# Three edits to a post-norm transformer layer: half order in the first projection slab, attention writes by quarters, smaller loads

## The chip, the cores and the metric

One Trainium2 chip, all 8 cores. The metric is the time of the slowest core in microseconds (us). Each core works on its own data: one of 4 sequences, and half of its query rows. No data passes between cores.

## What is computed

The reference, cut to its core (4 sequences of 4096 rows, width 4096, 32 heads of 128, 8 KV heads, 8 LoRA adapters of rank 16):

```python
q = (x @ Wq + bq); k = (x @ Wk + bk); v = (x @ Wv + bv)      # k, v repeated 4 times over heads
scores = einsum('bhqd,bhkd->bhqk', q, k) / sqrt(128) + causal_mask
attn   = einsum('bhqk,bhkd->bhqd', softmax(scores), v)
x = layernorm(x + attn @ Wo + bo)
h = einsum('bsd,nrd->nbsr', x, lora_A)
x = layernorm(x + x @ W.T + bias + einsum('nbsr,nor->bso', h, lora_B * coef))
```

## The kernel before

The kernel is raw code without a scheduler: each operation is written down once for its engine with the operations that it depends on, and each engine runs its operations in the order in which they were written. That holds for DMA issues too. An engine (SP, ACT or GpSimd, which the profile calls POOL) that issues a DMA first waits in its own queue for what the DMA depends on, and all that is queued behind it waits as well. A phase (`ir.phase`) begins on every engine only when the last operation of each engine and of each DMA channel of the phases before has finished. PE is TensorE, DVE is VectorE.

*Projection stage* (`gen_gemm`, L246 to L341). It is run for K and V over two groups of 2048 rows of x, and then once for Q over the core's 2048 query rows. A group of x (`x_bf`, 128 x 32 x 2048 in bf16) is loaded by GpSimd's queue in two halves of 1024 rows, 16 loads each (L259). The loads of a half wait for the last matmul that read the same half of the group before (`pe_last_half`, L255), and at most four are in flight. Weights come in slabs of four chunks (512 columns) into one buffer `w_bf`, in 8 loads (L284), queued behind the x loads of the group. K and V have four slabs, Q has eight. Odd groups run the slabs in reverse order, so that the first slab of the second K/V group is the last of the first and isn't loaded again. PE's work on a slab is a list of pairs (chunk, half), L294 to L298. Each pair is a pass over 32 row chunks of the contraction, with 2 matmuls of 128x512 for each, 64 in all. In most slabs the two halves follow each other within a chunk. In the last slab of a group all chunks of half 0 come first, so that the loads of the next group's half 0 can start.

*Attention stage* (L350 to L534). Four q blocks `qt` of 512 rows, for each of them 32 heads, for each head `NK = 8 * (qt + 1)` key chunks `kc`. A step is one score matmul (L466), the exponential on ACT (L471), for the last 8 chunks a mask multiply on DVE (L478), and, three steps late (`LAG = 3`), the matmuls with V (L452) and for the denominator (L455). A head's last three V matmuls therefore stand among the first three score matmuls of the next head. Two tails of each head run in the next one: after its third step the denominator is copied (L493) and inverted, and in the fifth step a matmul spreads it over the partitions (L506), ACT copies it (L510) and DVE multiplies it in (L514), into `aslab[:, h * 512:(h + 1) * 512]`.

SP's queue issues for this stage: the q load of each head (L433, two buffers, so that the load of head h + 2 waits for the last score matmul of head h), in q block 0 the K load of each of the 8 KV groups (L375, 1 MB), and the V chunks. These are loaded by a transposing DMA, one for each KV group and key chunk (L382), when they are first needed: 8 for each KV group in every q block, at the group's first head (0, 4, 8, ...). A transpose of one KV group waits for the transpose before it in that group (`vt_prev`). After a q block's last tail SP issues one write of all of `aslab` (4 MB) to `a_dram` (L528), then the mask (L414) and the q load of the next block. DVE's multiply into `aslab` waits for the last such write.

*Output stage* (L536 to L885), for two groups `tg` of 1024 query rows. `attnT` (8 MB) is loaded back in four loads of 2 MB (L664), and the first matmul (L680) waits for all four. The projection with Wo follows (L692), with residual, row sums and sums of squares, and a write of the sum to `r1_dram`. The first normalisation loads row blocks of 128 rows (2 MB, L740, two buffers), normalises them (L744) and transposes them on PE (L752). The LoRA and feed-forward matmuls (L771, L817, L824) follow, with a write to `r2_dram`. The second normalisation loads each row block in two halves of 1 MB from ACT's queue (L864), normalises each half (L873) and writes it to `y` (L879). Both belong to ACT's queue, so the loads of the next row block are issued only after both writes of this one, which wait for both multiplies.

Of the kernel before, what the change touches and what calls it, by code (L numbers as in the profile page):

```python
# [11 lines left out]
ALU = mybir.AluOpType  # L12
# [99 lines left out]
def build_program(cfg):  # L112
    T, D, H, KVH = cfg["T"], cfg["D"], cfg["H"], cfg["KVH"]
# [41 lines left out]
    ir = IR()  # L155
# [90 lines left out]
    def gen_gemm(src, gcount, gt, nsub, chunks, oc_base, same_layout=False):  # L246
# [5 lines left out]
        for gi in range(gcount):  # L252
# [21 lines left out]
            for slab in slabs:  # L274
# [16 lines left out]
                        for d in dset:  # L291
                            wc_ops[d] = ld
                new_lastuse = {}
                is_last_slab = (slab is slabs[-1])  # L294
                if is_last_slab:
                    pairs = [(ci, half) for half in range(halves) for ci in range(len(slab))]
                else:
                    pairs = [(ci, half) for ci in range(len(slab)) for half in range(halves)]  # L298
# [106 lines left out]
    rtmm_last = {}  # L405
    av_par = {}
    tail_prev = [None]
    slab_wr = [None]
    mask_last = [None]
    b_attn_done = None  # L410

    for qt in range(NQT):
# [17 lines left out]
        for h in range(H):  # L430
# [57 lines left out]
            def make_tails(h=h, hp=hp, stopv=stopv):  # L488
                carry = {}

                def tail1():
                    stopDen = stopv[1]
                    dc = ir.op("dve", lambda e, hp=hp: e.tensor_copy(  # L493
                        out=den_sb[hp][:], in_=ps_den[hp][:]), deps=[stopDen, lnlast.get(0)])
                    dclast[0] = dc
                    ln1 = ir.op("act", lambda e, hp=hp: e.activation(
                        out=rec_sb[hp][:], in_=den_sb[hp][:], func=AF.Ln), deps=[dc, rtmm_last.get(0)])
                    dr = ir.op("act", lambda e, hp=hp: e.activation(
                        out=rec_sb[hp][:], in_=rec_sb[hp][:], func=AF.Exp, scale=-1.0),
                        deps=[ln1])  # L500
                    lnlast[0] = dr
                    carry["dr"] = dr

                def tail2():
                    stopAV = stopv[0]
                    rt = pe_op(lambda e, hp=hp: e.matmul(  # L506
                        ps_rt[hp][:], orf_sb[:], rec_sb[hp][:], start=True, stop=True),
                        [carry["dr"], d_orf, rt_evac.get(0)])
                    rtmm_last[0] = rt
                    re = ir.op("act", lambda e, hp=hp: e.activation(  # L510
                        out=rt_sb[hp][:], in_=ps_rt[hp][:], func=AF.Identity),
                        deps=[rt, at_evac.get(0)])
                    rt_evac[0] = re
                    ae = ir.op("dve", lambda e, h=h, hp=hp: e.tensor_tensor(  # L514
                        out=aslab[:, h * 512:(h + 1) * 512], in0=ps_av[hp][:],
                        in1=rt_sb[hp][:], op=ALU.mult), deps=[stopAV, re, slab_wr[0]])
                    av_par[hp] = ae
                    at_evac[0] = ae
                return tail1, tail2
            t1, t2 = make_tails()  # L520
            tails.append([LAG, t1])
# [3 lines left out]
        for tset in tails:  # L525
            tset[1]()
        tails.clear()
        sw = ir.op("sp", lambda e, qt=qt: e.dma_start(  # L528
            out=a_dram[qt], in_=aslab[:]),
            deps=[av_par.get(0), av_par.get(1)], dma=True, chan="sw")  # L530
        slab_wr[0] = sw
        b_attn_done = sw
    freeall(psg)
    freeall(gb)  # L534

# [117 lines left out]
    for tg in range(NTG):  # L653
# [3 lines left out]
        for i in range(TSG):  # L657
            t, g = ps(f"psc{tg}_{i}", [128, 512]); pscg.append(g); psc.append(t)
        atld = []
        W2 = H * 512 // 2  # L660
        for qh in range(TG // 512):
            qt = tg * (TG // 512) + qh
            for hv in range(2):
                atld.append(ir.op("sp", lambda e, qt=qt, qh=qh, hv=hv: e.dma_start(  # L664
                    out=attnT[:, qh * H * 512 + hv * W2:qh * H * 512 + (hv + 1) * W2],
                    in_=a_dram[qt, :, hv * W2:(hv + 1) * W2]),
                    deps=[slab_wr[0], last_ffn_mm[0]],
                    dma=True, chan=f"atld{len(atld)}"))

        for oc in range(NOC):  # L670
# [66 lines left out]
        for ts in range(TSG):  # L737
            slot = ts % 2
            rows = tg * TG + ts * 128
            ld = ir.op("sp", lambda e, rows=rows, slot=slot: e.dma_start(  # L740
                out=rowbuf[slot][:], in_=r1_dram[rows:rows + 128, :]),
                deps=r1_done + rowbuf_user.get(slot, []), dma=True, chan=f"row{slot}")
            fin = ln1_fin
            xb = ir.op("dve", lambda e, ts=ts, slot=slot: e.tensor_scalar(  # L744
                out=x1row[:], in0=rowbuf[slot][:], scalar1=stat_rstd[:, ts:ts + 1],
                scalar2=stat_mb[:, ts:ts + 1], op0=ALU.mult, op1=ALU.add),
                deps=fin + [ld, x1row_waw[0]])
            rowbuf_user[slot] = [xb]
            lasttr = None
            for Dc in range(DC):  # L750
                i2 = ts * DC + Dc
                tr = pe_op(lambda e, Dc=Dc, i2=i2: e.transpose(  # L752
                    tp2[i2 % 2][:], x1row[:, Dc * 128:(Dc + 1) * 128], id_sb[:]),
                    [xb, d_id, x1f_ev.get(i2 - 2)])
                evv = ir.op("dve", lambda e, Dc=Dc, ts=ts, i2=i2: e.tensor_copy(
                    out=x1f[:, Dc * TG + ts * 128:Dc * TG + (ts + 1) * 128], in_=tp2[i2 % 2][:]),
                    deps=[tr])
                x1f_ev[i2] = evv
                lasttr = tr
            x1row_waw[0] = lasttr  # L760
# [98 lines left out]
        for ts in range(TSG):  # L859
            slot = ts % 2  # L860
            rows = tg * TG + ts * 128
            lds = []
            for hv in range(2):
                lds.append(ir.op("act", lambda e, rows=rows, slot=slot, hv=hv: e.dma_start(  # L864
                    out=rowbuf[slot][:, hv * D2:(hv + 1) * D2],
                    in_=r2_dram[rows:rows + 128, hv * D2:(hv + 1) * D2]),
                    deps=r2_done + [c2_xc_last[0]] + rowbuf_user.get(slot, []),
                    dma=True, chan=f"row{slot}" if hv == 0 else f"row{slot}b"))
            fin = ln2_fin
            oa2 = []  # L870
            for hv in range(2):
                osl = (ts * 2 + hv) % 3
                oa = ir.op("dve", lambda e, ts=ts, slot=slot, hv=hv, osl=osl: e.tensor_scalar(  # L873
                    out=outst[osl][:], in0=rowbuf[slot][:, hv * D2:(hv + 1) * D2],
                    scalar1=stat_rstd[:, ts:ts + 1],
                    scalar2=stat_mb[:, ts:ts + 1], op0=ALU.mult, op1=ALU.add),
                    deps=fin + [lds[hv]] + (outlast.get(osl) or []))
                oa2.append(oa)
                ow = ir.op("act", lambda e, rows=rows, hv=hv, osl=osl: e.dma_start(  # L879
                    out=y[rows:rows + 128, hv * D2:(hv + 1) * D2],  # L880
                    in_=outst[osl][:]),
                    deps=[oa], dma=True, chan=f"out{osl}")
                outlast[osl] = [ow]
                out_wr.append(ow)
# [65 lines left out]
```

How the kernel before makes its waits and increments, by code:

```python
                    def body(e, ids=ids):  # L95
                        waited = {}
                        for i in ids:
                            o = self.ops[i]
                            for d in o["deps"]:
                                p = self.ops[d]
                                if waited.get(p["sem"].num, -1) < p["val"]:
                                    e.wait_ge(p["sem"], p["val"])
                                    waited[p["sem"].num] = p["val"]
                            if o["fn"] is not None:
                                inst = o["fn"](e)
                                if o["sig"] or o["dma"]:
                                    inst.then_inc(o["sem"], 16 if o["dma"] else 1)
```

## Time and profile before

| | us |
|---|---|
| timed runs of before | 7345.82 and 7667.84, median 7506.83 |
| profiled execution | 7378.19 |
| its span, slowest core (core 3) | 7376.6 |
| spans of the other cores | 7326.0 to 7367.9 |
| PE busy in the span | 6164.9 (84%) |
| ACT, DVE, POOL busy | 2021.9, 915.7, 355.6 |

All shown rows are of core 3. The span runs from the first to the last instruction. The projection stage ends at about 2198, the q blocks begin at about 2199, 2545, 3010 and 3679, and attention ends at about 4570; the output stage of the first row group runs to about 6057.

### The profile page before, as it was taken

Reading aid. Unit: us, or ns where it says so; the run is one execution under the profiler, and the core shown is the slowest. Engines: PE = TensorE matmul, PEld = TensorE weight load, DVE = VectorE, ACT = ScalarE, POOL = GpSimd, SP = SyncE. Lnnn points to the kernel's source line nnn. Section 1 sums busy time; section 2 is a strip of 40 time slices with the busy share of each in tenths; the row PEclk is TensorE's granted clock in tenths of the full one; section 3 lists DMA queues with packets and bytes.
Section 4 is the critical chain, followed back from the end, with each engine's and each line's share of the span. In section 5 each row is a group of like instructions: output and inputs, shape, how many; then the busy total and the mean of one; then the engine's idle time right before and its main releaser. Section 6 shows DMA issues by size and latency. Waiting matters only on the chain.

```text
span 7376.6 us, 76089 instructions; the slowest of 8 cores (7326.0 to 7376.6 us)
## 1 busy us (share of the span) xinstructions
PE 6164.9 (84%) x25344; PEld 2271.1 (31%) x25344; DVE 915.7 (12%) x2390; ACT 2021.9 (27%) x3873; POOL 355.6 (5%) x480
## 2 busy tenths in 40 slices
PE   2988995999988899899999997789598849868883
PEld 0433442444432122222222221333243313323331
DVE  0000000000002222111111110111411111132111
ACT  0000000000014467677667775000011100001110
POOL 1001001000000000000000000000000000000000
PEclk9998997999996699999999998899699969978996
DMA  8246337323221100100000002666356696654667
GB/s 117 40 63 106 62 54 111 58 45 59 44 49 44 58 15 16 35 10 11 25 16 9 8 7 69 139 113 126 123 110 128 129 273 109 128 150 88 127 127 214
DMA packets 421434, 593.31 MB, mean 80 GB/s; under 512 B 75299, under 2 KB 316996, under 8 KB 408132
## 3 DMA queue, kind: packets, MB, share of 16 engines
q0 software_dynamic: 224704, 247.51, 24.7%
q10 hardware_dynamic: 101376, 201.37, 8.2%
q1 hardware_dynamic: 94980, 139.57, 5.7%
q8 instruction: 219, 3.59, 0.2%
q14 instruction: 155, 1.27, 0.1%
HBM read 676.42 MB, written 150.99 MB: 112 GB/s over the span
## 4 chain that ended last, share of the span: by engine, by line
PE 70%; DMA 20%; DVE 5%; issue 4%; SPq 0%; DVEq 0%; ACT 0%; ACTq 0%; POOL 0%; POOLq 0%
PE pa L309 18%; PE psd L817 12%; PE psd L692 10%; PE ps_den L455 9%; PE ps_s L466 9%; PE ps_av L452 7%; DMA w_bf<-wq 3%; DMA rowbuf<-r_scr 3%; DMA x_bf<-xt_kv 3%; DMA v_sb<-v_scr 2%; PE ps_rt L506 2%; DMA w_bf<-wk 2%; DMA w_bf<-wo 2%; DMA x_bf<-xt_q 1%; DMA w_bf<-wv 1%
## 5 line engine op out<-in xcount | busy, mean ns | idle before, releaser
L309 PE MATMUL pa<-x_bf,w_bf 128*128 128x512 bf16 x8192 | 1832.3, 386 | 361.6 <-DMA w_bf<-wk 167.1
L471 ACT ACTIVATE pt_sb<-ps_s 128x512 bf16<-128x512 f32 (+3 forms) x2560 | 1337.8, 531 | 615.8 <-PE ps_s L466 601.4
L309 PEld LDWEIGHTS pa<-x_bf,w_bf 128*128 128x128 bf16 x8192 | 804.4, 99 | 1389.0 <-issue 468.1
L452 PE MATMUL ps_av<-pt_sb,v_sb 128*128 128x512 bf16 (+3 forms) x2560 | 929.0, 363 | 109.2 <-DVE den_sb L493 85.7
L466 PE MATMUL ps_s<-q_sb,k_sb 128*128 128x512 bf16 (+3 forms) x2560 | 950.5, 372 | 62.9 <-DMA q_sb<-q_scr 48.9
L692 PE MATMUL psd<-w_bf,attnT 128*128 128x512 bf16 x4096 | 936.0, 392 | 46.7 <-DMA w_bf<-wo 46.4
L817 PE MATMUL psd<-w_bf,x1f 128*128 128x512 bf16 x4096 | 919.0, 388 | 4.9 <-DMA w_bf<-wff 4.8
L455 PE MATMUL ps_den<-pt_sb,ocol_sb 128*1 128x512 bf16 (+3 forms) x2560 | 912.5, 356 | 0.0
L478 DVE TENSOR_TENSOR pt_sb<-pt_sb,mask_sb 128x128 bf16<-128x128 bf16 x1024 | 230.1, 225 | 3619.9 <-ACT pt_sb L471 3614.6
L692 PEld LDWEIGHTS psd<-w_bf,attnT 128*128 128x128 bf16 x4096 | 408.0, 100 | 574.7 <-issue 129.0
L817 PEld LDWEIGHTS psd<-w_bf,x1f 128*128 128x128 bf16 x4096 | 405.8, 100 | 517.7 <-issue 59.5
L455 PEld LDWEIGHTS ps_den<-pt_sb,ocol_sb 128*1 128x1 bf16 x2560 | 202.5, 79 | 954.3 <-issue 951.6
L466 PEld LDWEIGHTS ps_s<-q_sb,k_sb 128*128 128x128 bf16 x2560 | 246.0, 96 | 674.6 <-issue 631.9
L714 ACT ACTIVATE scr_bf<-rst 128x512 bf16<-128x512 f32 x128 | 80.8, 631 | 1059.6 <-DVE rst L703 1052.0
L321 ACT ACTIVATE estage<-pa,bq_sb 128x512 bf16<-128x512 f32 x128 | 88.1, 688 | 966.4 <-PE pa L309 933.9
L844 ACT ACTIVATE scr_bf<-rst 128x512 bf16<-128x512 f32 x128 | 80.8, 631 | 901.7 <-DVE rst L833 897.3
L452 PEld LDWEIGHTS ps_av<-pt_sb,v_sb 128*128 128x128 bf16 x2560 | 254.6, 99 | 153.3 <-issue 152.2
L680 PE MATMUL psd<-bo_bc,orb_sb 1*128 1x512 bf16 x128 | 63.3, 517 | 234.1 <-DVE rst L703 130.3
L752 PE MATMUL tp<-id_sb,x1row 128*128 128x128 bf16 x512 | 106.7, 265 | 170.4 <-DVE x1row L744 89.6
L833 DVE TENSOR_TENSOR rst<-psd,xres 128x512 f32<-128x512 f32 x128 | 87.3, 682 | 964.3 <-PE psd L824 964.3
L703 DVE TENSOR_TENSOR rst<-psd,xres 128x512 f32<-128x512 f32 x128 | 87.3, 682 | 943.3 <-PE psd L692 935.3
L321 ACT ACTIVATE estage<-pa,bv_sb 128x512 bf16<-128x512 f32 x64 | 44.1, 689 | 470.6 <-PE pa L309 453.7
(62 smaller groups left out, 1758.5 us busy)
## 6 DMA issues: line engine op xcount, KB each, us to landing
w_bf<-wo POOLq DMA_DIRECT2D x128, 512.0 KB, 6.1
r_scr<-rst ACTq DMA_DIRECT2D x256, 256.0 KB, 7.2
w_bf<-wff POOLq DMA_DIRECT2D x128, 512.0 KB, 5.7
x_bf<-xt_kv POOLq DMA_DIRECT2D x64, 512.0 KB, 12.4
w_bf<-wq POOLq DMA_DIRECT2D x64, 512.0 KB, 7.7
xres<-x_q ACTq DMA_DIRECT2D x128, 256.0 KB, 6.4
rowbuf<-r_scr SPq DMA_DIRECT2D x16, 2048.0 KB, 8.5
xres<-r_scr SPq DMA_DIRECT2D x128, 256.0 KB, 7.9
```

Of the source, the lines that this page charges most:

```text
L309: mm = pe_op(lambda e, bank=bank, Dc=Dc, ci=ci, half=half, sub=sub, gt=gt, gth=gth: e.matmul(pa[bank][:], w_bf[:, Dc * 512 + ci * 128:Dc * ...
L321: act = ir.op("act", lambda e, bank=bank, slot=slot, bias_sb=bias_sb, bias_i=bias_i: e.activation(out=estage[slot][:], in_=pa[bank][:], fu ...
L452: av = pe_op(lambda e, kc=kc, kv=kv, par=par, hp=hp, NK=NK, s=s: e.matmul(ps_av[hp][:, s:512], v_sb[:, kc * DKV + kv * 128:kc * DKV + (kv ...
L455: dn = pe_op(lambda e, kc=kc, par=par, hp=hp, NK=NK, s=s: e.matmul(ps_den[hp][:, s:512], ocol_sb[:], pt_sb[par][:, s:512], start=(kc == 0) ...
L466: mm = pe_op(lambda e, kc=kc, kv=kv, par=par, hp=hp, s=s: e.matmul(ps_s[par][:, s:512], k_sb[:, kv * T + kc * 128:kv * T + (kc + 1) * 128] ...
L471: ex = ir.op("act", lambda e, par=par, s=s: e.activation(out=pt_sb[par][:, s:512], in_=ps_s[par][:, s:512], func=AF.Exp, scale=ISQ), deps= ...
L478: cur = ir.op("dve", lambda e, par=par, c=c, s=s: e.tensor_tensor(out=pt_sb[par][:, s:s + 128], in0=pt_sb[par][:, s:s + 128], in1=mask_sb[ ...
L506: rt = pe_op(lambda e, hp=hp: e.matmul(ps_rt[hp][:], orf_sb[:], rec_sb[hp][:], start=True, stop=True), [carry["dr"], d_orf, rt_evac.get(0)])
L692: mm = pe_op(lambda e, f=f, fi=fi, ts=ts, wi=wi, acol=acol: e.matmul(psc[ts][:], attnT[:, acol:acol + 128], w_bf2[wi % 2][:, fi * 512:(fi ...
L703: ev = ir.op("dve", lambda e, ts=ts, slot=slot: e.tensor_tensor(out=rst[slot][:], in0=psc[ts][:], in1=xres[slot][:], op=ALU.add), deps=[st ...
L752: tr = pe_op(lambda e, Dc=Dc, i2=i2: e.transpose(tp2[i2 % 2][:], x1row[:, Dc * 128:(Dc + 1) * 128], id_sb[:]), [xb, d_id, x1f_ev.get(i2 - 2)])
L817: mm = pe_op(lambda e, f=f, fi=fi, ts=ts, wi=wi: e.matmul(psc[ts][:], x1f[:, f * TG + ts * 128:f * TG + (ts + 1) * 128], w_bf2[wi % 2][:, ...
```

## The change

First, the first slab of a K/V group after the first, and of the Q group, is ordered like the last slab: all chunks of half 0, then all of half 1. Second, `aslab` is written in four quarters (8 heads, 1 MB each, each with its own channel). A quarter's write is issued by SP in the tail of its last head (7, 15, 23, 31), and the multiply waits only for the write of its own quarter. Third, three loads are cut: `attnT` into eight pieces instead of four, the row block of the first normalisation into two instead of one, and that of the second into four instead of two.

```diff
-                is_last_slab = (slab is slabs[-1])
-                if is_last_slab:
+                is_first_after = (slab is slabs[0]) and (gi > 0 or same_layout)
+                if (slab is slabs[-1]) or is_first_after:
                     pairs = [(ci, half) for half in range(halves) for ci in range(len(slab))]
                 else:
                     pairs = [(ci, half) for ci in range(len(slab)) for half in range(halves)]
...
-    slab_wr = [None]
+    swq = {}
+    slab_wr_q = {}
+    QD = max(H // 4, 1)
...
-                def tail2():
+                def tail2(qt=qt):
...
+                    qd = h // QD
                     ae = ir.op("dve", lambda e, h=h, hp=hp: e.tensor_tensor(
                         out=aslab[:, h * 512:(h + 1) * 512], in0=ps_av[hp][:],
-                        in1=rt_sb[hp][:], op=ALU.mult), deps=[stopAV, re, slab_wr[0]])
+                        in1=rt_sb[hp][:], op=ALU.mult), deps=[stopAV, re, swq.get(qd)])
                     av_par[hp] = ae
                     at_evac[0] = ae
+                    if h % QD == QD - 1:
+                        w = ir.op("sp", lambda e, qt=qt, qd=qd: e.dma_start(
+                            out=a_dram[qt, :, qd * QD * 512:(qd + 1) * QD * 512],
+                            in_=aslab[:, qd * QD * 512:(qd + 1) * QD * 512]),
+                            deps=[ae, swq.get(qd)], dma=True, chan=f"sw{qd}")
+                        swq[qd] = w
+                        slab_wr_q.setdefault(qt, []).append(w)
...
-        sw = ir.op("sp", lambda e, qt=qt: e.dma_start(
-            out=a_dram[qt], in_=aslab[:]),
-            deps=[av_par.get(0), av_par.get(1)], dma=True, chan="sw")
-        slab_wr[0] = sw
-        b_attn_done = sw
+        b_attn_done = slab_wr_q[qt][-1]
...
-        W2 = H * 512 // 2
+        W2 = H * 512 // 4
...
-            for hv in range(2):
+            for hv in range(4):
                 atld.append(ir.op("sp", lambda e, qt=qt, qh=qh, hv=hv: e.dma_start(
...
-                    deps=[slab_wr[0], last_ffn_mm[0]],
+                    deps=slab_wr_q[qt] + [last_ffn_mm[0]],
...
-            ld = ir.op("sp", lambda e, rows=rows, slot=slot: e.dma_start(
-                out=rowbuf[slot][:], in_=r1_dram[rows:rows + 128, :]),
-                deps=r1_done + rowbuf_user.get(slot, []), dma=True, chan=f"row{slot}")
+            lds = []
+            for hv in range(2):
+                D2 = D // 2
+                lds.append(ir.op("sp", lambda e, rows=rows, slot=slot, hv=hv, D2=D2: e.dma_start(
+                    out=rowbuf[slot][:, hv * D2:(hv + 1) * D2],
+                    in_=r1_dram[rows:rows + 128, hv * D2:(hv + 1) * D2]),
+                    deps=r1_done + rowbuf_user.get(slot, []), dma=True,
+                    chan=f"row{slot}" if hv == 0 else f"row{slot}b"))
...
-                deps=fin + [ld, x1row_waw[0]])
+                deps=fin + lds + [x1row_waw[0]])
...
-            for hv in range(2):
-                lds.append(ir.op("act", lambda e, rows=rows, slot=slot, hv=hv: e.dma_start(
-                    out=rowbuf[slot][:, hv * D2:(hv + 1) * D2],
-                    in_=r2_dram[rows:rows + 128, hv * D2:(hv + 1) * D2]),
+            D4 = D // 4
+            for qv in range(4):
+                sub = "bcd"[qv - 1] if qv else ""
+                lds.append(ir.op("act", lambda e, rows=rows, slot=slot, qv=qv: e.dma_start(
+                    out=rowbuf[slot][:, qv * D4:(qv + 1) * D4],
+                    in_=r2_dram[rows:rows + 128, qv * D4:(qv + 1) * D4]),
                     deps=r2_done + [c2_xc_last[0]] + rowbuf_user.get(slot, []),
-                    dma=True, chan=f"row{slot}" if hv == 0 else f"row{slot}b"))
+                    dma=True, chan=f"row{slot}{sub}"))
...
-                    deps=fin + [lds[hv]] + (outlast.get(osl) or []))
+                    deps=fin + lds[2 * hv:2 * hv + 2] + (outlast.get(osl) or []))
```

The second edit moves instructions in SP's queue. The piece below is of q block 0, from the K load of heads 8 to 11 on. Before:

```order
L375 DMA k_sb<-k_scr 128x4096
L382 DMA_TRANSPOSE v_sb<-v_scr 128x128 x5
L433 DMA q_sb<-q_scr 128x512
L382 DMA_TRANSPOSE v_sb<-v_scr 128x128 x3
L433 DMA q_sb<-q_scr 128x512 x3
L375 DMA k_sb<-k_scr 128x4096
```

And with the change, where the line numbers are two higher and L523 is the new write:

```order
L375 DMA k_sb<-k_scr 128x4096
L382 DMA_TRANSPOSE v_sb<-v_scr 128x128 x2
L523 DMA a_scr<-aslab 128x4096
L382 DMA_TRANSPOSE v_sb<-v_scr 128x128 x3
L435 DMA q_sb<-q_scr 128x512
L382 DMA_TRANSPOSE v_sb<-v_scr 128x128 x3
L435 DMA q_sb<-q_scr 128x512 x3
```

The write of heads 0 to 7 stands between the second and the third of the eight V transposes of the KV group that begins with head 8. The q load behind the next three transposes is that of head 9.

In q block 1, from the transposes of heads 4 to 7 to those of heads 8 to 11, SP's queue before:

```order
L382 DMA_TRANSPOSE v_sb<-v_scr 128x128 x5
L433 DMA q_sb<-q_scr 128x512
L382 DMA_TRANSPOSE v_sb<-v_scr 128x128 x3
L433 DMA q_sb<-q_scr 128x512 x3
L382 DMA_TRANSPOSE v_sb<-v_scr 128x128 x5
L433 DMA q_sb<-q_scr 128x512
```

And with the change:

```order
L382 DMA_TRANSPOSE v_sb<-v_scr 128x128 x5
L435 DMA q_sb<-q_scr 128x512
L382 DMA_TRANSPOSE v_sb<-v_scr 128x128 x3
L435 DMA q_sb<-q_scr 128x512 x3
L523 DMA a_scr<-aslab 128x4096
L382 DMA_TRANSPOSE v_sb<-v_scr 128x128 x5
L435 DMA q_sb<-q_scr 128x512
L382 DMA_TRANSPOSE v_sb<-v_scr 128x128 x3
```

Here the write stands ahead of all eight transposes, because only key chunks 8 to 15 are new in this block. The last of the three q loads ahead of it is that of head 8, and the same holds at heads 16 and 24, and in q blocks 2 and 3. At the end of a q block the order is as before, with a quarter of `aslab` in place of the whole.

## Rows read from the trace of the kernel before

**Rows 1.** The page's first line, and its waits of one group of matmuls (part 5).

```profile
span 7376.6 us, 76089 instructions; the slowest of 8 cores (7326.0 to 7376.6 us)
...
L466 PE MATMUL ps_s<-q_sb,k_sb 128*128 128x512 bf16 (+3 forms) x2560 | 950.5, 372 | 62.9 <-DMA q_sb<-q_scr 48.9
```

**Rows 2.** Timeline from 587 us (start, us, engine, line, op; idle before and its releaser).

```profile
587.46 0.69 ACT L321 ACTIVATE estage<-pa,bv_sb 128x512 bf16<-128x512 f32 x1 [11.87 <-PE pa L309]
...
601.27 0.69 ACT L321 ACTIVATE estage<-pa,bv_sb 128x512 bf16<-128x512 f32 x1 [11.87 <-PE pa L309]
...
629.63 0.71 POOL L259 DMA_DIRECT2D x_bf<-xt_kv  x1 [6.26 <-PE pa L309]
...
643.95 1.02 PE L309 MATMUL pa<-x_bf,w_bf 128*128 128x512 bf16 x4 [0.25 <-DMA x_bf<-xt_kv]
...
690.83 89.07 PE L309 MATMUL pa<-x_bf,w_bf 128*128 128x512 bf16 x404 [0.60 <-DMA x_bf<-xt_kv]
```

**Rows 3.** Timeline of SP's queue, q block 0, transposes of heads 8 and 16.

```profile
2281.83 14.98 SPq L382 DMA_TRANSPOSE v_sb<-v_scr  x5
...
2298.03 5.63 SPq L382 DMA_TRANSPOSE v_sb<-v_scr  x3
...
2364.65 12.76 SPq L382 DMA_TRANSPOSE v_sb<-v_scr  x5
```

**Rows 4.** Timeline of DVE and PE in the same stretch.

```profile
2300.17 0.69 DVE L514 TENSOR_TENSOR aslab<-ps_av,rt_sb 128x512 bf16<-128x512 f32 x1 [1.44 <-ACT rt_sb L510]
...
2304.94 0.26 PE L452 MATMUL ps_av<-pt_sb,v_sb 128*128 128x128 bf16 x1 [0.50 <-DMA v_sb<-v_scr]
```

**Rows 5.** Timeline of SP's queue, q blocks 1, 2 and 3 (first and last of a head).

```profile
2662.43 10.14 SPq L382 DMA_TRANSPOSE v_sb<-v_scr  x5
2675.43 0.32 SPq L433 DMA_DIRECT2D q_sb<-q_scr  x1
...
2690.69 27.14 SPq L433 DMA_DIRECT2D q_sb<-q_scr  x3
...
3184.47 0.33 SPq L433 DMA_DIRECT2D q_sb<-q_scr  x1
...
3204.64 40.65 SPq L433 DMA_DIRECT2D q_sb<-q_scr  x3
...
3908.09 0.33 SPq L433 DMA_DIRECT2D q_sb<-q_scr  x1
...
3935.01 55.66 SPq L433 DMA_DIRECT2D q_sb<-q_scr  x3
```

**Rows 6.** Timeline of DVE, the normalising multiply of heads 7 in q blocks 1 and 2.

```profile
2682.22 0.69 DVE L514 TENSOR_TENSOR aslab<-ps_av,rt_sb 128x512 bf16<-128x512 f32 x1 [3.73 <-ACT rt_sb L510]
...
3190.68 0.69 DVE L514 TENSOR_TENSOR aslab<-ps_av,rt_sb 128x512 bf16<-128x512 f32 x1 [3.52 <-ACT rt_sb L510]
```

**Rows 7.** Timeline around the end of q block 0.

```profile
2546.30 8.24 SPq L433 DMA_DIRECT2D q_sb<-q_scr  x1
...
2559.27 1.86 PE L466 MATMUL ps_s<-q_sb,k_sb 128*128 128x512 bf16 x4 [15.44 <-DMA q_sb<-q_scr]
```

**Rows 8.** A window after that end: stretch, us, busy by engine, PEclk, DMA share, GB/s.

```profile
2559.00:2565.00 6.00, 5.73 (x13) 1.10 (x14) 0.00 (x0) 3.26 (x6) 0.00 (x0) 0.51 0.05 11
```

**Rows 9.** DMA issues (part 6): line, count, KB each, median us to landing.

```profile
rowbuf<-r_scr SPq DMA_DIRECT2D x16, 2048.0 KB, 8.5
...
k_sb<-k_scr SPq DMA_DIRECT2D x8, 1024.0 KB, 5.9
```

**Rows 10.** Chain that ended last, end of the attention stage: start, us, what.

```profile
4569.86 12.58 DMA a_scr<-aslab
```

**Rows 11.** Timeline of the last normalising stage, first row blocks.

```profile
7262.22 0.81 ACTq L864 DMA_DIRECT2D rowbuf<-r_scr  x2
7268.83 1.35 DVE L873 TENSOR_SCALAR outst<-rowbuf,stat_rstd,stat_mb 128x2048 f32<-128x2048 f32 x1 [7.17 <-DMA rowbuf<-r_scr]
...
7271.99 1.35 DVE L873 TENSOR_SCALAR outst<-rowbuf,stat_rstd,stat_mb 128x2048 f32<-128x2048 f32 x1 [1.81 <-DMA rowbuf<-r_scr]
```


## The prediction

> **What bounds the kernel now.** I read the page first, then the waits, the chain that ended last, and the timeline at each place where the chain leaves TensorE (PE). PE is the bound nearly everywhere in a span of 7376.6 us [rows 1]. A change that leaves every matmul in place can win only where PE stands still, and lose only where it makes PE stand still. The reader is to see four such places. (a) In the projection stage PE waits for the second half of the next x: it begins that half's first matmuls at 643.95 and meets the last load at 690.83 [rows 2]. (b) At each of the three changes of q block PE waits for the first q. One of the three waits is 15.44 us [rows 7], and together they make nearly all of the 48.9 that this group waits for q [rows 1]. (c) The attention stage ends with one write of 4 MB, 12.58 us on the chain [rows 10]. (d) Both normalising stages at the end of a token group run at the pace of loads and stores [rows 11].
>
> The fifth place is one where PE does not wait today. SP's queue carries the q loads, the K loads, the transposed V loads and the attention writes in one line. In a group of four heads it runs a head ahead: in q block 1 the five transposes of head 8 start at 2662.43, while the head's own scores begin only about 2675.4 [rows 5].
>
> **The change part by part.** All is summed on the profiled execution's 7378.19 us (span 7376.6), which lies between the two timed runs, 7345.82 and 7667.84, whose median is 7506.83.
>
> *First slab by halves.* One pass (a chunk of one half, 64 matmuls) takes 601.27 - 587.46 = 13.81 us [rows 2]. Before, PE starts the half-1 pass at 643.95 and needs until 690.83 + 1.7 = 692.5, the last load's four matmuls included. With the change three more half-0 passes come first, 643.9 to 685.3, and the half-1 pass then runs to 699.1. The last load's matmuls are due at the end of that pass, at 698.2, 7 us after it has landed. The stall 692.5 - 643.95 - 13.8 = 34.7 us is gone; nothing is late next. The same order at the start of the Q projection gives nothing. There the weight loads stand behind all 32 x loads in GpSimd's queue, so no pass can start before both halves of x are loaded or on their way. I take 35 us, bounds 30 to 35.
>
> *Writes by quarters, at the ends of q blocks.* The first q of the next block no longer queues behind 4 MB but behind 1 MB, plus the mask. 4 MB take 12.58 us [rows 10], 1 MB takes 5.9 us as the K loads show [rows 9]: 6.7 us less. By the slope alone (12.58 / 4 = 3.1 us a MB) it would be 9.4. Three changes of block at 7 us give 21 (bounds 15 to 29), and the end of the stage gives 6.7 (5 to 9.4).
>
> *Writes by quarters, inside a q block.* The writes after heads 7, 15 and 23 of every block now stand in SP's line behind a wait for the multiply of that head (L514), which comes in the fifth step of heads 8, 16 and 24. Each of these heads is the first of a new KV group, so behind the waiting write stand the group's V transposes, six of eight in q block 0 and all eight in the others, and between them the q load of the next head. A transpose waits for the one before, five in 10.14 us, 2.05 each [rows 5]. Behind a 1 MB K load in the same queue five took 14.98 and 12.76 [rows 3], so 1 MB ahead costs 2.6 to 4.8 us. I take 3.7 for the write.
>
> - q block 0: L514 ends at 2300.86 [rows 4]; write issued by 2301.3; three transposes 3 x 2.05 + 3.7, to 2311.1. From the end of the fifth transpose (2281.83 + 14.98) to the end of the last three (2298.03 + 5.63) are 6.85 us [rows 3], so 2318.0. PE took the last V at 2304.94, 1.3 after its issue ended [rows 4]; now it is 2319.3. Stall 14.3 us.
> - q block 1: L514 ends at 2682.91 [rows 6]; transposes from 2683.3; 10.14 + 3.7, q load 0.4, three more 5.7, landing 1.3: 2704.5. The head's scores ended at 2690.69 [rows 5] and the last V is due three steps later, at 2693.2 (a step is (3935.01 - 3908.09) / 32 = 0.84 us). Stall 11.3.
> - q block 2: L514 ends at 3191.37, 6.9 after the head's start at 3184.47 [rows 5, 6]; the same 21.2 us from 3191.8 give 3213.0. Due at 3204.64 + 2.5 = 3207.1. Stall 5.9.
> - q block 3: the same offset gives 3908.09 + 7.3 + 21.2 = 3936.6, due at 3937.5. No stall, 0.9 us of cover.
>
> Three each: 3 x 31.5 = 94.5 us. While PE is paced by the transposes it is mostly idle, and after an idle stretch its clock is low: in the 6 us after the wait at 2559.27 the granted clock is 0.51 of full, 1.2 GHz [rows 7, 8], 6 x 0.49 = 2.9 us lost. Six stalls in blocks 1 and 2 add 17; block 0 is often at the low level anyway (0 to 9 there). In all 112 us, bounds 85 (3.7 replaced by 2.6, no lost clock) to 131.
>
> *Smaller loads.* attnT comes in eight pieces instead of four, and its first matmul still waits for all; the row loads of the first normalisation are prefetched two deep behind PE's transposes; both 0. In the second normalisation each half row block now comes as two pieces. The trace does not show such a piece. Two loads of 1 MB issued together in 0.81 us landed so that the multiplies began at 7268.83 and 7271.99, 3.2 us apart [rows 11]: the second paid bandwidth only, no start of its own, and four pieces move the same bytes. I take 0. Two more issues of 0.4 us for each of 16 row blocks, if none is hidden, cost 13; an earlier first piece might gain 0.5 each, 8.
>
> The Trainium skill ("DMA: Bandwidth & Descriptors", section "Anatomy of one DMA") has a fixed part of about 2 us per DMA plus bytes over 436 GB/s, measured on GpSimd's path. Were it paid one after another, 32 more pieces would add an estimated 64 us; rows 11 speak against it, since two loads in flight overlap it.
>
> Sum: 7378.2 + 112 - 35 - 21 - 7 + 0 = 7427, 0.7% more. About 2% is what a measurement of this kernel tells from no change, so this is "the same".
>
> **The rivals.**
> - *The writes hide, as meant.* If SP's wait cost PE nothing, the gains alone remain: 7378 - 63 = 7315. For it: no wait for V is among the releasers that the page names for its costliest groups. Against it: rows 5 and 6 leave 8 us from L514 to the end of the head in block 1, and eight transposes need 16 even unhindered.
> - *The half order gives nothing,* because x loads beside full-rate matmuls slow down, or PE's order is bound otherwise: 7462. Against it: 7 us of slack.
> - *The slower side: pieces pay their own start in the second normalisation.* Its place is the chain of 16 row blocks, where ACT's queue issues the next loads only after both multiplies of the block before. 1 MB in 5.9 and 2 MB in 8.5 us [rows 9] make 3.3 us of start. If a piece's start were not overlapped, two more per block cost 16 x 2 x 3.3 = 106: 7533, 2.1% slower. It decides from 3.1 us per added piece. Rows 11 speak against it.
>
> **How the numbers follow.** Forecast 7427 with 0.70; its own range, all costs low and all gains high 7382, the reverse 7472. Hidden writes 0.12, no gain of the halves 0.07, starts not overlapped 0.06, and 0.05 for mixtures. I name 7425. The range 7310 to 7520 takes in the forecast's own range and the first two rivals; the last rival lies just outside. Its upper end leaves 48 us above the own range, because the two runs of before alone spread by 4.4%. Faster by over 2% needs 7231, below every case: 0.02. Slower by over 2% is the last rival and some of the mixtures: 0.08. Within 2%: 0.90.
>
> **What would show it.** The wait of ps_av (L452) for v_sb, small now, must grow to the order of 90 us, with its longest single wait near heads 8, 16 and 24 of block 0, falling from block 0 to 2 and absent in block 3. In SP's queue the write's issue must follow L514 directly, with an empty stretch of some 20 us ahead of it in block 1. The wait of ps_s for q must fall from 48.9 to about 28. The chain must show no x load from about 640 to 690, the next slab must start some 35 us earlier, and the Q projection must be unchanged. The row-block period of the last stage must stay as it is. If the V wait stays below 30 us the sum is wrong on its largest term; if the period rises by 3 us, the slower rival holds.

## The result, and the profile after

| | runs | lowest us | median us | ratio to before [95%] |
|---|---|---|---|---|
| before, same chip | 11 | 7344.57 | 7634.65 | |
| changed | 13 | 7397.19 | 7705.91 | 1.0072 [1.0044, 1.0100] |

The change costs 0.7%; by the 2% bound this is "the same". The forecast ratio was 7427 / 7378.2 = 1.0066. The measured median, 7705.91, lies outside the stated range of 7310 to 7520. Many executions of either kernel give one die's four cores a lower granted clock, which lifts the medians; the ratios, spans and stage times below leave those executions and cores out.

Line numbers are two or three higher than before in the attention stage (L454 for L452, L468 for L466, L517 for L514; L523 is the new write). Of the profiled execution core 3 is read (span 7399.5 us; cores 0 to 3 have 7375.4 to 7405.4). Its largest waits, with columns: waiting instruction, what ended the wait, us in all, count, longest:

```profile
PE ps_av L454 <- DMA v_sb<-v_scr: 92.1, 68, 6.6
...
PE ps_s L468 <- DMA q_sb<-q_scr: 31.9, 13, 8.2
```

In before the wait for q was 48.9 [rows 1], and that for V stood far down the list:

```profile
PE ps_av L452 <- DMA v_sb<-v_scr: 22.1, 21, 1.7
```

The prediction wanted "the order of 90" and "about 28". The work itself has not changed: PE is busy 6191.4 us.

SP's queue around the write after head 7, in q block 1 (start, us, queue, line, op):

```profile
2659.50 0.32 SPq L523 DMA_DIRECT2D a_scr<-aslab  x1
2659.91 12.68 SPq L382 DMA_TRANSPOSE v_sb<-v_scr  x5
2672.68 0.52 SPq L435 DMA_DIRECT2D q_sb<-q_scr  x1
2673.98 5.65 SPq L382 DMA_TRANSPOSE v_sb<-v_scr  x3
```

And what DVE and PE do there (the bracket is the idle time before, and its releaser):

```profile
2658.72 0.69 DVE L517 TENSOR_TENSOR aslab<-ps_av,rt_sb 128x512 bf16<-128x512 f32 x1 [3.79 <-ACT rt_sb L512]
...
2671.58 0.48 PE L454 MATMUL ps_av<-pt_sb,v_sb 128*128 128x384 bf16 x1 [2.49 <-DMA v_sb<-v_scr]
...
2680.91 0.27 PE L454 MATMUL ps_av<-pt_sb,v_sb 128*128 128x128 bf16 x1 [1.27 <-DMA v_sb<-v_scr]
```

Read it from DVE down: the multiply of head 7 ends at 2659.41, SP issues the write 0.1 later, and only then do the eight transposes run that before had run a head earlier [rows 5]. PE gets the last V 21.5 us after the multiply; the prediction had 21.6 (2682.91 to 2704.5). This is the mechanism: the wait ahead of the write holds back V, and the write itself adds a part that e5 sizes.

In q block 0 two transposes escape ahead of the write, as the order of instructions said:

```profile
2233.91 6.19 SPq L382 DMA_TRANSPOSE v_sb<-v_scr  x2
...
2248.43 0.33 SPq L523 DMA_DIRECT2D a_scr<-aslab  x1
2248.85 7.19 SPq L382 DMA_TRANSPOSE v_sb<-v_scr  x3
2256.13 0.51 SPq L435 DMA_DIRECT2D q_sb<-q_scr  x1
2257.23 5.70 SPq L382 DMA_TRANSPOSE v_sb<-v_scr  x3
```

At a block's end the first q now waits less behind the write (8.21 us here, 15.44 in [rows 7]), and the stage's last write is followed 4.3 us later by the first load of the next stage, where it was 12.7:

```profile
2538.35 1.87 PE L468 MATMUL ps_s<-q_sb,k_sb 128*128 128x512 bf16 x4 [8.21 <-DMA q_sb<-q_scr]
```

```profile
4614.61 0.32 SPq L523 DMA_DIRECT2D a_scr<-aslab  x1
4618.91 0.87 SPq L583 DMA_DIRECT2D rowbuf<-at  x1
```

A table by stage says more than the spans. A q block runs here from one mask load's issue to the next in SP's queue (block 3 to the first load of the output stage); each figure is the median over the cores of one profile. "Slab" is the first slab of the second K/V group, from the last PSUM evacuation (ACT, L321) of the slab before to its own.

| us | slab | projection, to | block 0 | 1 | 2 | 3 |
|---|---|---|---|---|---|---|
| before | 149.1 | 2196 | 346.5 | 465 | 672 | 903.5 |
| changed | 110.5 | 2142 | 382 | 506.5 | 696 | 885 |
| e1, half order alone | 112.0 | 2148 | 345 | 464 | 672 | 902 |
| e2, quarter writes alone | 148.8 | 2190 | 377 | 507 | 695.5 | 886 |
| e3, smaller loads alone | 148.9 | 2189 | 345.5 | 465 | 672 | 905 |
| e4, writes from GpSimd | | 2142 | 341 | 447 | 658 | 887 |
| e5, wait, little data | | | 373 | 515 | 697 | 906 |
| e6, writes deferred | | | 344 | 455 | 665 | 886 |
| e7, half order at K/V alone | 111.5 | 2154 | 343.5 | 463 | 672.5 | 900 |
| e8, half order, GpSimd writes | 114.2 | 2177 | 342 | 449 | 657 | 887 |

What is left, the output stage, is 2759 in before, 2764 in e1, 2773 in e7, 2775 in e8 and 2788 in e2, all with the same loads, and 2781 in the changed kernel. A difference of 20 us there can't be read from one profile.

### The profile page after: what moved, and what is told of

It reads as the page before. It is cut to its first block, busy times and chain, and to the rows that moved or that the text cites. A ratio compares the mean times of both kernels' runs of the same rounds, so it can differ in the third digit from the quotient of the medians.

```text
span 7582.1 us, 76241 instructions; the slowest of 8 cores (7375.4 to 7582.1 us)
## 1 busy us (share of the span) xinstructions
PE 6434.6 (85%) x25344; PEld 2336.5 (31%) x25344; DVE 920.6 (12%) x2390; ACT 2017.9 (27%) x3873; POOL 355.7 (5%) x480
## 4 chain that ended last, share of the span: by engine, by line
PE 73%; DMA 16%; DVE 5%; issue 3%; ACTq 1%; ACT 0%; SPq 0%; DVEq 0%; POOL 0%; POOLq 0%
PE pa L309 22%; PE psd L828 12%; PE psd L698 11%; PE ps_den L457 9%; PE ps_s L468 9%; PE ps_av L454 6%; DMA v_sb<-v_scr 3%; DMA w_bf<-wq 3%; DMA rowbuf<-r_scr 2%; PE ps_rt L508 2%; DMA w_bf<-wk 2%; DMA x_bf<-xt_kv 1%; DMA w_bf<-wv 1%; DVE den_sb L495 1%; DVE rst L709 1%
## 5 line engine op out<-in xcount | busy, mean ns | idle before, releaser
L309 PE MATMUL pa<-x_bf,w_bf 128*128 128x512 bf16 x8192 | 2056.0, 421 | 285.5 <-DMA w_bf<-wk 154.9
L309 PEld LDWEIGHTS pa<-x_bf,w_bf 128*128 128x128 bf16 x8192 | 861.7, 106 | 1479.3 <-issue 1175.2
L454 PE MATMUL ps_av<-pt_sb,v_sb 128*128 128x512 bf16 (+3 forms) x2560 | 936.4, 366 | 177.9 <-DMA v_sb<-v_scr 89.9
L468 PE MATMUL ps_s<-q_sb,k_sb 128*128 128x512 bf16 (+3 forms) x2560 | 962.1, 377 | 45.1 <-DMA q_sb<-q_scr 34.4
L468 PEld LDWEIGHTS ps_s<-q_sb,k_sb 128*128 128x128 bf16 x2560 | 247.1, 97 | 667.2 <-issue 625.3
L321 ACT ACTIVATE estage<-pa,bq_sb 128x512 bf16<-128x512 f32 x128 | 87.9, 687 | 998.2 <-PE pa L309 965.7
L454 PEld LDWEIGHTS ps_av<-pt_sb,v_sb 128*128 128x128 bf16 x2560 | 255.7, 100 | 238.8 <-issue 237.6
L321 ACT ACTIVATE estage<-pa,bv_sb 128x512 bf16<-128x512 f32 x64 | 44.0, 687 | 508.9 <-PE pa L309 491.9
```

Of the source, the lines that this page charges most:

```text
L309: mm = pe_op(lambda e, bank=bank, Dc=Dc, ci=ci, half=half, sub=sub, gt=gt, gth=gth: e.matmul(pa[bank][:], w_bf[:, Dc * 512 + ci * 128:Dc * ...
L321: act = ir.op("act", lambda e, bank=bank, slot=slot, bias_sb=bias_sb, bias_i=bias_i: e.activation(out=estage[slot][:], in_=pa[bank][:], fu ...
L454: av = pe_op(lambda e, kc=kc, kv=kv, par=par, hp=hp, NK=NK, s=s: e.matmul(ps_av[hp][:, s:512], v_sb[:, kc * DKV + kv * 128:kc * DKV + (kv ...
L468: mm = pe_op(lambda e, kc=kc, kv=kv, par=par, hp=hp, s=s: e.matmul(ps_s[par][:, s:512], k_sb[:, kv * T + kc * 128:kv * T + (kc + 1) * 128] ...
```

## The experiments

**e1, the half order alone.** The first two lines of the diff, the rest as before.

> The kernel before with the half order alone. My theory: the projection stage ends 35 us earlier (the stall on the second half of x goes) and all that follows keeps its length, so about 35 us or 0.5% less than before. The changed kernel's profile shows the stage 47 us shorter on core 3, and where it is cut by another 12 us is open: a rival says that the half order also shortens the start of the Q projection (then the first weight-paced pass or the wait before it is shorter here too, total 47 less); another says that those 12 us were only the loads' luck in that execution (then 35 here). A third rival, no gain at all from the half order: the stage keeps its length and the other edits made the gain.

The best of its four runs took 7297.81 us, the best of before's 13 beside them 7345.89: 48 us, from too few runs for a ratio. By die (the median span of a die's four cores, then the median of these over the dies of all runs) it is 7292 against 7331, 39 us. The slab falls from 149.1 to 112.0 and the blocks stay within 1.5 us. The end of the projection moves by 48 (2196 to 2148), but e2 and e3, with the old order, have 2190 and 2189, so 6 or 7 of it belong to before's execution. The half order gives 37 in its slab; some 4 us more in the projection aren't placed.

**e7, where it gives.** Only the K/V part: `is_first_after = (slab is slabs[0]) and gi > 0`.

> The kernel before with the half order for the second K/V group only, not for the Q group. My theory: the whole gain is in that one slab, which falls from 149 to 112 us; the first slab of Q stays at 192 to 195 us and the projection stage ends 37 to 42 us earlier than before. The rival that the Q group gains too expects the stage to end 5 to 10 us later than with both.

The slab is 111.5, as with the whole edit. The first slab of Q takes 195.1, which is before's 195.1; with the edit at Q too it takes 191.8 (e1) and 191.2 (changed), without it 193.0 (e2) and 191.6 (e3). So at Q nothing is to be seen. For the total e7 says little: its best run, 7356.15 us, is no faster than the best of before beside it, 7348.62, while by die it takes 7315 against 7346.

**e2, the quarter writes alone.** The second edit; order of the slabs and loads as before.

> The kernel before with the quarter writes alone. My theory: three waits of SP in each q block hold back the V transposes: q block 0 about 33 to 43 us longer, block 1 about 36 to 42, block 2 about 20 to 26, block 3 about 7 to 10 shorter, the end of the stage 7 to 8 shorter; in all about 75 to 100 us or 1.0 to 1.35% more than before. The rival that the writes hide and the loss comes from the other edits expects 28 us less than before, 0.4%.

Ratio 1.0148 [1.0093, 1.0204]. The blocks show what it costs: +30.5, +42, +23.5 and -17.5, together +79 of the 109 us that the ratio names. The expectation had 75 to 100. The ratio's interval, 68 to 150 us, holds the blocks' 79; the other 30 would stand in the output stage, where the spread above doesn't resolve them.

**e5, the wait without the data.** As e2, but the writes after heads 7, 15 and 23 carry 16 rows of one head (16 KB), and the whole 4 MB goes out at the block's end.

```diff
-    out=a_dram[qt, :, qd * QD * 512:(qd + 1) * QD * 512],
-    in_=aslab[:, qd * QD * 512:(qd + 1) * QD * 512]),
+    out=a_dram[qt], in_=aslab[:]) if qd == 3 else e.dma_start(
+    out=a_dram[qt, 0:16, qd * QD * 512:qd * QD * 512 + 512],
+    in_=aslab[0:16, qd * QD * 512:qd * QD * 512 + 512]),
...
```

> The kernel before, but after heads 7, 15 and 23 SP waits for the multiply and then writes only 16 rows of 512 values (16 KB) in place of a quarter; the whole slab is written at the block's end as before. It parts the wait from the data. By the prediction's sum the data ahead of the transposes costs 3.7 of each stall of 14.3, 11.3 and 5.9 us, so the waits alone give 10.6, 7.6 and 2.2: with the time at low clock in blocks 1 and 2 (2.9 each) and the write at the block's end unchanged, q block 0 is 32 us longer than before, block 1 31, block 2 15, block 3 the same. If the data and not the wait is the cause, all four blocks keep their length of before (346, 465, 672, 903 us).

The blocks grow by 26.5, 50, 25 and 2.5, where the expectation had 32, 31, 15 and 0: the wait alone costs nearly all, and more than expected in blocks 1 and 2. Since the block ends keep their 4 MB (the wait for q is 54.3 us between 2200 and 4560, 31.3 in the changed kernel), these are the costs of the waits alone. The changed kernel, with 7 us for the shorter wait at the start of blocks 1 to 3 and 8 for the end of the stage added back, has 35.5, 48.5, 31 and -3.5. The differences, 9, -1.5, 6 and -6, scatter too much to show the price of the megabytes. No ratio could be formed for e5 (best run 7583.39 us); by die it takes 7456, before 7346 beside it.

SP's queue shows that price better. One piece of it in block 1, behind a 16 KB write:

```profile
2701.63 0.33 SPq L524 DMA_DIRECT2D a_scr<-aslab  x1
2702.05 11.93 SPq L382 DMA_TRANSPOSE v_sb<-v_scr  x5
2714.07 0.52 SPq L435 DMA_DIRECT2D q_sb<-q_scr  x1
2715.17 5.78 SPq L382 DMA_TRANSPOSE v_sb<-v_scr  x3
```

This piece alone, 11.93 against 12.68 with 1 MB and 10.14 with nothing ahead [rows 5], would say that any write costs and its size hardly matters. All such pieces of the eight cores say otherwise. Medians in us of the transposes behind 1 MB (changed), behind 16 KB (e5) and behind a q load (before):

| | 1 MB | 16 KB | none |
|---|---|---|---|
| block 0, three transposes | 7.22 | 5.71 | 5.67 |
| block 1, five | 13.02 | 11.92 | 10.26 |
| block 2, five | 12.51 | 10.30 | 10.51 |
| block 3, five | 11.94 | 10.65 | 10.88 |

The megabyte costs 1.1 to 2.2 us. The small write costs 1.7 in block 1 and nothing in the others.

**e4, the same writes from another queue.** The changed kernel with one word changed, `ir.op("sp"` to `ir.op("pool"` for the write.

> The changed kernel with the quarter writes issued by GpSimd, whose queue holds nothing else in the attention stage, instead of SP. If the loss comes from SP's wait and from what stands behind it in its queue, q blocks 0 to 2 fall back below their lengths of before (about 346, 458 and 662 us between the ends of blocks) and the total is about 110 us under the changed kernel, about 0.8% under the kernel before. If the 1 MB of data beside the transposes and loads costs the time, whatever queue it is in, the blocks stay 26 to 42 us longer than before and the total is that of the changed kernel.

The best of six runs took 7275.54 us; cores 0 to 3 of the profile have spans of 7235.8 to 7263.4. By die it is 7249 against 7331, 1.1% under before, where 0.8% was expected. SP's queue in q block 1 is as before [rows 5], a head ahead:

```profile
2643.70 0.32 SPq L435 DMA_DIRECT2D q_sb<-q_scr  x1
2644.11 10.15 SPq L382 DMA_TRANSPOSE v_sb<-v_scr  x5
```

The write is issued by GpSimd, where nobody waits behind it:

```profile
2330.65 0.55 POOL L523 DMA_DIRECT2D a_scr<-aslab  x1 [85.44 <-DVE pt_sb L480]
```

Waits for V and q between 2200 and 4560 us, core 3, in the changed kernel:

```profile
PE ps_av L454 <- DMA v_sb<-v_scr: 86.1, 62, 6.6
PE ps_s L468 <- DMA q_sb<-q_scr: 31.3, 12, 8.2
```

and with GpSimd's queue:

```profile
PE ps_av L454 <- DMA v_sb<-v_scr: 17.5, 13, 2.5
PE ps_s L468 <- DMA q_sb<-q_scr: 2.6, 2, 1.8
```

With 1 MB writes in flight at the same places the wait for V is as small as before. So neither the bandwidth nor the write itself makes the stall: the place of the write in SP's queue does. The q wait goes too, which I had not put in the prediction: the next block's q, mask and V no longer stand behind SP's wait for the last multiply.

**e6, the writes later in SP's own queue.** The quarter of heads 0 to 7 is issued in the tail of head 10, and so on; the last one stays at the block's end.

```diff
-                    if h % QD == QD - 1:
+                    wd = qd if h == H - 1 else (qd - 1 if h % QD == 2 and qd > 0 else None)
+                    ael[qd] = ae
+                    if wd is not None:
...
```

> The changed kernel with the same 1 MB quarter writes on SP's queue, but those of heads 7, 15 and 23 are issued three heads later (in the tail of heads 10, 18, 26), where the multiply they wait for has long ended and the next V transposes are still to come. If the wait is the cause, the blocks lose their excess: about 340, 458 and 664 us for blocks 0 to 2, as with the writes on GpSimd's queue plus the 6 us at each block's end that the last quarter on SP costs; the total is about 90 us under the changed kernel. If 1 MB in SP's ring costs the time wherever it stands, each of the three still costs 3 to 5 us and more where it delays the next head's q load: the excess falls only by half or less.

Two runs, 7656.25 and 7825.87 us, from which no ratio could be formed. The blocks are 344, 455, 665 and 886, the last two from the four cores of one die. That is before's 346.5, 465, 672 and 903.5 less the gain of the ends, and 340, 458 and 664 were expected for the first three. The wait for V falls to 22.8 us. The writes need not leave the queue; it is enough that they stand where their multiply is long done and no transpose is behind them. For the whole there is one die only, in the second run: 7286 us, 60 under before's 7346, in the same reading as e8's 7276.

**e3, the smaller loads alone.** The third edit.

> The kernel before with the smaller loads alone (attnT in 8, the row loads of the first normalisation in 2, of the second in 4). My theory from the prediction: 0, with bounds of 8 less to 13 more. The changed kernel's profile has the time from the end of attention to the end 22 us shorter on core 3, of which 8 belong to the last write: so the rival that smaller loads gain expects about 14 us less, in the second normalisation. The slower rival of the prediction expects 106 us more, in the same place.

Ratio 1.0038 [0.9996, 1.0080], slabs and blocks as before. That excludes the 14 us less of the one rival (0.998) and the 106 more of the other (1.014).

**e8, the parts that gain.** Half order, quarter writes from GpSimd, loads as before.

> The version that should beat both: half order and quarter writes on GpSimd's queue, with the loads as in the kernel before. Projection 37 to 47 us shorter, q blocks about 341, 447, 658 and 887 us (5, 18, 14 and 16 shorter, as in the run with the writes on GpSimd's queue), the rest as before: 90 to 100 us or 1.25% under the kernel before. If the small loads had carried part of the gain, it stays above that by their part.

Ratio 0.9885 [0.9835, 0.9936], best of six runs 7269.63 us. It is faster than both kernels, clear of noise though by less than 2%. Its slab falls by 35 us and its blocks by 52 (342 + 449 + 657 + 887 against 2387), together 87, where the ratio says 84. The projection as a whole ends only 19 us earlier, not the 37 to 47 expected; what takes back the rest there isn't known.

**e9, with the smaller loads again, and e10, one of them alone.** e9 is the same program as e4, in more runs; e10 is before with only the second normalisation's loads in four pieces.

> The version that issues the quarter writes from GpSimd's queue, with the half order and with all the smaller loads of the changed kernel: the same program as the fourth experiment, timed now in more rounds. Theory 1 (smaller loads are worth nothing either way): the ratio to before is that of the version with whole loads, 0.9885, within 0.002; the row-block period of the last normalising stage is 12.8 to 13.6 us. Theory 2 (each added piece of a load pays a part of its own start): the ratio is 0.993 or more. Theory 3 (they gain, by first operands that arrive earlier): 0.985 or less.

> Before, with one edit: in the second normalisation each row block's load comes in four pieces where it came in two (32 more DMAs in all). Theory 1 (nothing): ratio 1.000 within 0.002, period per row block within 0.4 us of before's 12.8. Theory 2 (each piece pays part of a start): the slower side rival of the prediction was 6.6 us per row block, 106 us in all or 1.014; the 0.4 us per block that the profiles so far cannot exclude would be 6 us or 1.001.

e9: 0.9919 [0.9889, 0.9950], between its first and its second theory and not to be told from e8's 0.9885. e10: 1.0019 [0.9997, 1.0041], which holds "nothing" and some 6 us alike, but not 106. The stage shows more than the ratios, since it can be summed over ten profiles: from the first row block's load to the first issue to `y` of the last row block, both row groups together, mean of eight cores. With two pieces: 229.7 (before), 228.8 (e1), 231.5 (e7), 234.2 (e8), 236.2 (e2). With four: 237.1 (changed), 239.4 (e3), 238.4 (e10), 235.7 (e4), 236.8 (e9). The means are 232.1 and 237.5: 5.4 us for 16 row blocks, 0.34 each. How firm that is the pairs tell: e3 and e10 lie 9 to 10 above before, but e4 and e9 only 2 to 3 above e8, and the changed kernel 1 above e2. ACT's queue shows where such a cost could come from. In before, core 3, the issues of two loads:

```profile
7273.79 1.45 ACTq L864 DMA_DIRECT2D rowbuf<-r_scr  x2
7288.28 1.38 ACTq L864 DMA_DIRECT2D rowbuf<-r_scr  x2
```

and of four, in the changed kernel, with the multiplies that follow the first row:

```profile
7302.98 3.26 ACTq L877 DMA_DIRECT2D rowbuf<-r_scr  x4
7316.38 3.23 ACTq L877 DMA_DIRECT2D rowbuf<-r_scr  x4
```

```profile
7311.62 1.35 DVE L886 TENSOR_SCALAR outst<-rowbuf,stat_rstd,stat_mb 128x2048 f32<-128x2048 f32 x1 [9.10 <-DMA rowbuf<-r_scr]
...
7314.53 1.35 DVE L886 TENSOR_SCALAR outst<-rowbuf,stat_rstd,stat_mb 128x2048 f32<-128x2048 f32 x1 [1.55 <-DMA rowbuf<-r_scr]
```

Two more issues take 1.8 us of the queue, 29 us for 16 row blocks; as the stage grows by 5, most of it must be hidden, and the runs don't show that the rest is the cause. From one row block's loads to the next are 14.49 us in before and 13.40 in the changed kernel in these rows, so the period hasn't grown here. The second multiply starts 2.9 us after the first. A piece with a start of its own of 3.3 us would have made the second multiply come over 6 us after it.

## Why the prediction was right or wrong

The forecast of the change was right: 1.0066 against 1.0072 [1.0044, 1.0100], and the mechanism is the one it named. That the two agree to 4 us is partly luck. By the profiles the projection is 54 us shorter (forecast 35), the blocks 82.5 longer (forecast 84) and the output stage 22 longer (forecast 0): two deviations of about 20 us cancel, neither larger than what profiles of the same code differ by (projection 2148 in e1 and 2177 in e8, output stage 2759 in before and 2788 in e2). What was wrong was the range in microseconds. By steps:

- **Half order, -35:** measured -37 in the slab (e1, e7). Right, and right that Q gives nothing; but the bounds of 30 to 35 were too tight. On core 3 before, the granted clock is 0.50 from 650 to 692 and 0.61 in the 3 us after, and 1.00 throughout the same slab in the changed kernel. The sum had the idle time of that stall and no term for the clock; whether that makes the 2 us, the rows don't say.
- **Block ends, 3 x 7, and the stage's end, 6.7:** the wait for q fell by 17.0 us (48.9 to 31.9), 15.44 to 8.21 at the first end, and the end of the stage by 8.4. Right: 17.0 and 8.4 lie inside the bounds of 15 to 29 and 5 to 9.4.
- **Mid-block writes, +112:** the stalls fall from block to block and vanish in block 3, as worked out. With the ends taken in, the steps give +43, +36, +19 and -14, in all +84; measured +35.5, +41.5, +24 and -18.5, in all +82.5. Two sizes inside were off, in opposite directions, and that the sum came out so near is luck too. *The write's own price* of 3.7 us, taken from 1 MB K loads, was too high: five transposes behind it took 12.68, so 2.5, and in block 0 three took 7.19, only 1.0 over 3 x 2.05; this makes block 0 cheaper than said, by 2.7 us in each of three places. *The lost clock* of 2.9 us a stall was too low. The last V was due 10.3 us after the multiply and came 21.5 after it, a stall of 11.2; a group costs (41.5 + 7) / 3 = 16.2. That leaves 5.0. The window rows show it (start:end, us, busy by engine, PEclk, DMA share, GB/s):

```profile
2664.00:2671.00 7.00, 4.10 (x16) 1.02 (x14) 1.36 (x6) 2.63 (x6) 0.00 (x0) 0.99 0.08 16
2671.00:2687.00 16.00, 10.28 (x23) 2.44 (x24) 0.91 (x2) 4.39 (x9) 0.00 (x0) 0.50 0.10 25
2681.00:2691.00 10.00, 9.61 (x19) 1.69 (x18) 1.37 (x2) 4.55 (x8) 0.00 (x0) 0.50 0.03 11
```

  The last V comes at 2680.91, and the clock stays at 0.50, 1.2 GHz, until about 2691: 10 us of nearly unbroken work at half speed, where the term had 6; half of 10 is the 5.0. In all six stalls of blocks 1 and 2 on this core the clock is low until 31 to 33 us after the multiply, and the last V comes 21 to 23 after it. It is low within the stall too; there PE waits for V in any case, so nothing is counted for it.
- **Smaller loads, 0:** ratio 1.0019 for the one that the slower rival was about; its 106 us (1.014) lies far outside [0.9997, 1.0041]. The stage's sums give some 5 us, within the -8 to +13 of the prediction, though two more issues take 1.8 us and not 2 x 0.4. The Trainium skill ("DMA: Bandwidth & Descriptors", section "Anatomy of one DMA") has about 2 us fixed per DMA, measured on GpSimd's path, while these loads are issued by ACT. Paid one after another, 32 more of them would be an estimated 64 us by that page; e10's interval ends at 30 us, and the stage's sums give 5, so loads in flight together do not add it up here.
- **The rivals:** "the writes hide" fell (e2: V waits for the queue). "The half order gives nothing" fell (e1). "Pieces pay their own start" fell (e10).
- **How the numbers follow, the range:** this step failed. All was summed on an execution at 7378, near the bottom of before's spread, although the median on record was 7506.83; that median times 1.0066 is 7556, already above the range's upper end of 7520. And the upper end was set 48 us above the forecast's own range "because the two runs of before alone spread by 4.4%", but that spread is 322 us, and 48 does not cover it. The runs showed in its place a median of 7705.91 for the changed kernel, and for before itself 7634.65, over 11 runs between 7344.57 and 7979.53. A range for a median must hold where the median may fall for an unchanged kernel. The two known runs times 1.0066, 7394 to 7718, would have held it, by 12 us.

Not settled: the 30 us of e2's ratio that no block shows, why e8's projection gains only 19 us, and what the smaller loads are worth: e3 and e10 lie 0.4% and 0.2% above before with intervals that include no change, while e9 and e8, which differ by them, overlap.

## What to carry to other kernels

A DMA's issue that waits for a computation is a wait for everything behind it in that queue, so splitting a store to start it earlier can cost more than it gains: here the split paid 7 to 8 us at each end and lost 11 to 16 at each early piece in the first three q blocks, since a chain of transposed loads stood behind it, and nothing in the fourth, where the heads are long enough. Ask of each moved issue what the queue would have been doing, and put such stores in a queue with nothing urgent behind them (e8, -1.2%) or later, where their operand is long finished (e6). And when a program's runs spread by 8%, state the change as a ratio and give the microseconds the width of the spread.

## What the hardware showed that I had not expected

A 16 KB write ahead of the transposing loads cost them nothing in three of four q blocks and 1.7 us in the other, a 1 MB write 1.1 to 2.8 us in every block (table in e5). PE's granted clock was 0.50 in the last 10 us of the waits, and the 10 us of nearly unbroken work behind the last of them ran at 0.50 too, so that an 11 us stall cost 16. And three quarters of the 4 MB less took only 17 of the 48.9 us of waits for q; with the write in another queue 2.6 were left. What remains between them is the last megabyte and SP's wait for the block's last multiply, ahead of which no q could be issued; the runs don't part the two.
